# Attention in an 8-expert layer: score passes over 64 keys of two heads, in three units, with the masks as products on GpSimd

## The chip, the core and the metric

The kernel runs on one core of a Trainium2 chip. The core has five engines that work side by side and meet only in semaphores: TensorE (matmuls, results in PSUM banks), ScalarE (activations and copies), VectorE (element-wise work and reductions), GpSimd (element-wise work on SBUF and the indirect DMAs) and SyncE (the queue of plain DMAs). Each works through its own list in order, so an instruction that waits holds up all that stand behind it on its engine. The metric is the device time of one execution in microseconds.

## The reference

One transformer layer on 16 sequences of 256 tokens of width 128: normalised input, causal linear attention with 16 heads, a residual, and a mixture of 8 experts of which each token takes 2 (where both chosen experts have a positive weight, the one with the higher number gives the output). Attention goes in chunks of 64 with a running state, but since the features are all products of two components of q or k, it is the same as a full causal attention with the square of q.k as weight:

```
q = q * f ** (-0.5)
A = jnp.einsum('bhcf,bhsf->bhcs', qi, ki) ** 2 * mask
o = (inter_o + intra_o) / (inter_z + intra_z + EPS)[..., None]   # inter: the same squares over earlier chunks
x = x + attention(layernorm(x)) @ Wo
x = x + experts(layernorm(x))      # gate logits, softmax, top 2 of 8, relu(x w1 + b1) w2 + b2
```

The kernel uses this form: square every score, set those of later keys to zero, multiply by the values extended by a column of ones, and divide by that column.

## The kernel before

**Stages.** First attention for 16 batches (sequences), one a period; then a stage of 39 tiles of 128 rows through the experts. The loop `for p in PERIODS` stands in every engine's code, and each engine takes in it the batches that are its turn: `new` = p is projected, `core` = p-1 is scored, `late` = p-2 is finished and divided, `tail` = p-3 gets its output projection and residual. Pairs of batches are routed: logits when p-4 is even (even periods), the choice when p-5 is even (odd periods), and `scatter` sends a batch's rows to its experts' regions in memory at p-6. No scheduler moves anything: the order of each engine's list is as written.

**Scores.** The 16 heads are two halves (`gg`) of 8; in each, four strips of 32 partitions hold two heads of 16 features, and `k_sb` exists twice, with the features of the one or of the other head set to zero. `score_group(b, g)` (L1085) is one half and one of the two heads of a strip: for each of four strips, 128 keys against 256 queries, and the later 128 keys against the later 128 queries, 384 columns a strip, into the four PSUM banks `sc`. There is one set of those banks: the next group waits in `after(pe, squared, ...)` until ScalarE's `square` (L409) has taken them to SBUF. `mask` (L560) on GpSimd zeroes in 256 of each strip's 384 columns what lies after the query. `weigh` (L1106), A V, adds the four groups into the bank `av`; the first two run in the batch's own period, the last two in the next.

**Around them.** TensorE's list of a period is: scores 0, `project_o(tail)`, `project_q(new)`, scores 1, A V of the batch before (two groups), scores 2, `project_k`, `prefix` (running counts per expert, odd periods), `project_v`, `transpose_xn`, scores 3, two groups of A V. VectorE's is: statistics of two batches ahead (`norm1_stats`, even periods), `residual` and `norm2_stats` of `tail`, the choice, `norm1_apply`, `spread` (a transpose of `av`), `divide` (den, rden, o_sb, oT), `part_k`, `gate_x`, and then either places and slots (odd) or logits, ahead and best (even). GpSimd's is: four masks, with a root (`norm1_root` or `norm2_root`, an addition and a power by -0.5) and two `scatter` DMAs between them. The bank `p7` holds the projected values, the output projection and the counts in turn.

## Time and profile before

| | |
|---|---|
| time, median of 3 runs | 287.44 us (286.88 to 288.08) |
| span of the profiled execution, first to last instruction | 266.1 us |
| outside the span, to the median | 21.3 us |
| TensorE busy | 246.5 us (93%) |
| VectorE busy | 198.0 us (74%) |
| ScalarE busy | 169.0 us (64%) |
| GpSimd busy | 165.9 us (62%) |
| 64 squares on ScalarE | 92.8 us |
| 64 masks on GpSimd | 71.1 us |

The profiled execution has no time of its own beside its span; the 21.3 us are what lies around the span if that execution took the median. Attention fills the span to about 164 us and the experts the rest from about 179. A busy share is an average over stages, and TensorE's includes matmuls that stream beside each other; what a stage is bound by is read from who waits there. A duration includes what an instruction stood for after it had begun.

### The profile page before, as it was taken

What the parts mean: (1) busy time and instruction counts of PE and PEld (TensorE: products, weight loads), DVE (VectorE), ACT (ScalarE), POOL (GpSimd) and SP (SyncE); (2) the same over time, 40 slices, a digit from 0 to 9 for tenths busy, and PEclk for the clock granted to TensorE, in tenths of its full rate; (3) what the DMA queues carried; (4) which work ended last, traced back from release to release, by engine and by line L of the source; (5) the groups of instructions that cost most, each with busy time, mean ns of one, the idle gap of its engine ahead of it and who ended that gap; (6) DMA issues with size and microseconds to landing.
All of it is one profiled execution on the core that took longest, in us unless ns stands there. A gap on an engine that the chain in (4) does not pass through costs nothing.

```text
span 266.1 us, 9039 instructions
## 1 busy us (share of the span) xinstructions
PE 246.5 (93%) x3072; PEld 198.4 (75%) x3072; DVE 198.0 (74%) x715; ACT 169.0 (64%) x311; POOL 165.9 (62%) x190
## 2 busy tenths in 40 slices
PE   6998999999999999999999998887999999999993
PEld 2676777777776776776677766545989999999992
DVE  4877466786899899899799798669888655555552
ACT  2687776776867777677767767534555665656640
POOL 6265555555876976878766766850577774545455
PEclk9999999999999999999999999999999999999998
DMA  3589999999950000000000000447766479776310
GB/s 86 167 254 309 366 358 360 357 357 354 358 164 23 18 5 24 10 14 23 2 23 21 2 23 22 136 124 177 191 179 186 140 245 271 212 182 202 109 39 10
DMA packets 31692, 40.58 MB, mean 153 GB/s; under 512 B 3442, under 2 KB 24468, under 8 KB 31648
## 3 DMA queue, kind: packets, MB, share of 16 engines
q1 hardware_dynamic: 29376, 35.76, 44.3%
q0 software_dynamic: 2272, 4.25, 4.6%
q8 instruction: 26, 0.43, 0.7%
q14 instruction: 18, 0.15, 0.2%
HBM read 17.98 MB, written 22.48 MB: 152 GB/s over the span
## 4 chain that ended last, share of the span: by engine, by line
PE 64%; ACT 17%; DVE 7%; POOL 5%; issue 4%; DMA 1%; DVEq 1%; POOLq 0%
PE sc L1080 32%; PE p L1080 22%; ACT scores L413 16%; PE av L1080 8%; PE p L1083 3%; POOL expert_rows L591 2%; POOL scores L563 2%; DVE hT L1008 1%; DMA rows<-in_L_attn_hidden_states 1%; POOL out L604 1%; DVE y_sb L1014 0%; DVE logit L764 0%; DVE scaled L762 0%; DVE y_sb L1020 0%; POOL rstd L580 0%
## 5 line engine op out<-in xcount | busy, mean ns | idle before, releaser
L413 ACT ACTIVATE scores<-sc 128x1536 f32<-128x1536 f32 x64 | 92.8, 1451 | 44.8 <-PE sc L1080 44.5
L563 POOL TENSOR_SCALAR_AFFINE_SELECT scores<-scores 128x1024 f32<-128x1024 f32 x64 | 71.1, 1113 | 45.2 <-ACT scores L413 44.5
L1080 PE MATMUL sc<-q_sb,k_sb 32*128 32x256 f32 (+1 forms) x1024 | 59.8, 347 | 9.2 <-ACT scores L413 4.9
L1080 PEld LDWEIGHTS sc<-q_sb,k_sb 32*128 32x128 f32 x1024 | 47.8, 184 | 26.5 <-issue 16.6
L604 POOL DMA_INDIRECT out<-y_sb,xr x39 | 38.5, 987 | 26.1 <-DVE y_sb L1020 21.8
L1080 PE MATMUL av<-scores,v_ext 128*32 128x256 f32 (+1 forms) x1024 | 48.8, 329 | 0.3 <-POOL scores L563 0.2
L513 ACT ACTIVATE hT<-sc,b_sb 128x128 f32<-128x128 f32 x78 | 24.4, 363 | 32.9 <-PE sc L1080 32.9
L1080 PE MATMUL sc<-xwT,w_t 128*128 128x128 f32 x312 | 41.6, 276 | 0.0
L1080 PEld LDWEIGHTS av<-scores,v_ext 128*32 128x32 f32 x1024 | 28.9, 109 | 15.8 <-POOL scores L563 1.0
L1008 DVE TENSOR_SCALAR hT<-sc,b_sb 128x128 f32<-128x128 f32 x78 | 23.8, 347 | 20.9 <-PE sc L1080 18.3
L591 POOL DMA_INDIRECT expert_rows<-rows,slot_i x32 | 32.8, 1024 | 9.9 <-issue 7.3
L1080 PEld LDWEIGHTS sc<-xwT,w_t 128*128 128x128 f32 x312 | 37.9, 192 | 0.1
L1080 PE MATMUL av<-w_sb,hT 128*128 x160 | 22.3, 283 | 0.0
L1080 PE MATMUL p<-w_sb,hT 128*128 x152 | 20.6, 279 | 0.0
L1080 PEld LDWEIGHTS av<-w_sb,hT 128*128 128x128 f32 x160 | 19.4, 191 | 1.3 <-issue 0.2
L506 ACT ACTIVATE xw<-xr 128x128 f32<-128x128 f32 x39 | 19.8, 510 | 0.6 <-DMA xr<-expert_rows 0.6
L1080 PEld LDWEIGHTS p<-w_sb,hT 128*128 128x128 f32 x152 | 18.4, 191 | 0.5
L1080 PE MATMUL p<-xnT,wk_sb 128*128 128x256 f32 x62 | 17.6, 406 | 0.6 <-ACT xnT L425 0.6
L663 DVE TENSOR_SCALAR xn<-rows,mv,rstd 128x128 f32<-128x128 f32 x32 | 16.1, 545 | 2.4 <-POOL rstd L572 2.2
L712 DVE STREAM_TRANSPOSE u_sb<-av 128x512 f32<-128x512 f32 x16 | 11.4, 713 | 7.6 <-PE av L1080 7.5
L1080 PE MATMUL p<-xnT,wq_sb 128*128 128x256 f32 x62 | 16.2, 382 | 0.0
L690 DVE TENSOR_SCALAR k_sb<-p,parity 128x512 f32<-128x512 f32 x15 | 11.1, 738 | 5.8 <-ACT k_sb L436 5.8
(147 smaller groups left out, 333.5 us busy)
## 6 DMA issues: line engine op xcount, KB each, us to landing
expert_rows<-pad_rows SPq DMA_DIRECT2D x11, 1572.0 KB, 17.9
w_t<-in_L_ffn_w SPq DMA_DIRECT2D x39, 256.0 KB, 3.2
xr<-expert_rows SPq DMA_DIRECT2D x39, 65.5 KB, 2.5
rows<-in_L_attn_hidden_states SPq DMA_DIRECT2D x16, 128.0 KB, 2.7
out<-y_sb,xr POOLq DMA_INDIRECT x39, 3.3
b_sb<-in_L_ffn_b SPq DMA_DIRECT2D x1, 512.0 KB, 5.7
expert_rows<-rows,slot_i POOLq DMA_INDIRECT x32, 2.4
wk_sb<-in_L_attn_Wk SPq DMA_DIRECT2D x1, 128.0 KB, 2.5
```

The lines of the kernel that those rows point to most:

```text
L413: nc.scalar.activation(scores[g][:, :, :, :].rearrange("p c a t -> p c (a t)"), sc[:, :, 0:SW], ACT.Square, scale=Q_SCALE).then_inc(square ...
L506: nc.scalar.activation(xw[t % 2][:, :], xr[t % XR][:, 0:D], ACT.Identity, bias=xr[t % XR][:, MEAN:MEAN + 1], scale=xr[t % XR][:, FACTOR:FA ...
L513: ins = nc.scalar.activation(hT[t % HT][:, c * P:(c + 1) * P], up_bank[t % 2][0][:, c * P:(c + 1) * P], ACT.Relu, bias=b1_sb[:, bass.ds(e ...
L563: nc.gpsimd.affine_select(out=scores[g][:, :, 0:2, :], in_=scores[g][:, :, 0:2, :], compare_op=ALU.is_ge, fill=0.0, base=0, pattern=[[0, G ...
L591: nc.gpsimd.indirect_dma_start(out=region, out_offset=bass.IndirectOffsetOnAxis(ap=slot_i[:, b, j:j + 1], axis=0), in_=rows[:, b, j, :], i ...
L604: nc.gpsimd.indirect_dma_start(out=out.rearrange("b l d -> (b l) d"), out_offset=bass.IndirectOffsetOnAxis(ap=xr[t % XR][:, IDCOL:IDCOL + ...
L663: ins = nc.vector.tensor_scalar(xn[b % 2][:, j, :], rows[:, b, j, 0:D], mv1[:, b, j, 0:1], rstd1[:, b, j:j + 1], ALU.subtract, ALU.mult)
L690: nc.vector.tensor_scalar(k_sb[b % 2][1][:, :], p5[:, :], parity[:, 1:2], None, ALU.mult).then_inc(k_ready[1], 1)
L712: nc.vector.transpose(u_sb[:, :, :, :, :].rearrange("p n g r w -> p g n (r w)"), av[:, :].rearrange("p (g n w) -> p g n w", g=NG, w=STRIP) ...
L1008: ins = nc.vector.tensor_scalar(hT[t % HT][:, c * P:(c + 1) * P], up_bank[t % 2][1][:, at:at + P], b1_sb[:, bass.ds(e * FC + c, 1)], 0.0, ...
L1080: return nc.tensor.matmul(o, lhsT=l, rhs=r, start=start, stop=stop)
L1083: return nc.tensor.transpose(o, i, ident[:, :])
```

## The change

- A pass of scores has on its 128 partitions 64 keys of one head and the same 64 keys of the strip's other head, instead of 128 keys of one head. `k_sb` holds both heads' keys side by side per chunk of 64, and `v_ext` has the values of the one head in the upper 64 partitions and of the other in the lower.
- The rows of a batch are stored rolled by 64, so that the chunk order in memory is 1, 2, 3, 0 (`PLACE`); `MEETS` lists the stretch of queries that each chunk of keys meets: 256, 192, 128 and 64 columns. A strip has 640 columns per half instead of 768.
- Three units of scores a batch instead of four groups: 448 columns (half 0, chunks 0, 3, 2), 384 (chunk 1 of both halves), 448 (half 1). The tiles of units 0 and 1 exist twice, that of unit 2 once.
- A V of a batch is one piece, in the next period, between scores 1 and scores 2.
- The mask is a product with `causal`, a 128 x 64 tile of ones and zeros, over the diagonal 64 x 64 blocks only: 768, 512 and 768 elements a partition.
- `project_o` moves from behind scores 0 of the next period to the end of its own, into bank `p5` (the last two batches into `p7`); `project_k` follows `project_q`. `residual` and `gate_x` are first on VectorE, logits come before `part_k`, `norm1_stats` later. Roots come first on GpSimd, scatters one period earlier.
- Values are projected in eight pieces of 64 partitions; `gate_x` and `place_v` work on halves. `Wo` and `Wv` are laid out before the call, and `Wo` comes in one DMA instead of eight.

```diff
@@ tiling @@
-    SW = L + P
+    CH = P // 2
+    NK = L // CH
+    PLACE = [(c - 1) % NK for c in range(NK)]
+    MEETS = [(0, L), (0, L - CH), (CH, L - CH), (2 * CH, L - CH)]
+    UNITS = [[(0, 0), (0, 3), (0, 2)], [(0, 1), (1, 1)], [(1, 0), (1, 3), (1, 2)]]
+    NU = len(UNITS)
+    WIDTH = [sum(MEETS[c][1] - MEETS[c][0] for _, c in unit) for unit in UNITS]
...
-        k_sb = [[sb(f"k_sb{i}{r}", [P, NG * L]) for r in range(2)] for i in range(2)]
-        v_ext = [sb(f"v_ext{i}", [P, NTK, 2, H // 2, STRIP]) for i in range(2)]
-        scores = [sb(f"scores{g}", [P, GH, 3, P]) for g in range(GROUPS)]
+        k_sb = [sb(f"k_sb{i}", [P, NG, NK, 2, CH]) for i in range(2)]
+        v_ext = [sb(f"v_ext{i}", [P, NK, H // 2, STRIP]) for i in range(2)]
+        scores = [[sb(f"scores{u}{i}", [P, GH, WIDTH[u]]) for i in range(2 if u < 2 else 1)] for u in range(NU)]
...
+        projected = [bank[:, 0:NTK * DE].rearrange("p (j d) -> p j d", j=NTK) for bank in (p5, p7)]
+        def output_bank(b):
+            return projected[0 if b < NB - 2 else 1]
...
-        CORE, LATE, TAIL, LOGITS, CHOICE, SEND = 1, 2, 3, 4, 5, 6
+        CORE, LATE, TAIL, LOGITS, CHOICE, SEND = 1, 2, 3, 4, 5, 5
@@ scalar @@
+            def square(b, u):
+                act.wait_ge(scored, NU * b + u + 1)
+                after(act, av_done, b - 1 if u < 2 else b)
+                nc.scalar.activation(unit(b, u)[:, :, :], sc[:, :, 0:WIDTH[u]], ACT.Square,
+                                     scale=Q_SCALE).then_inc(squared, 1)
...
                 square(core, 0)
-                if choice is not None:
-                    exponent(choice)
                 if new is not None:
                     copy_q(new)
+                    part_k(new)
                 square(core, 1)
+                if logits is not None and p < NB:
+                    exponent(logits)
                 square(core, 2)
-                if new is not None:
-                    part_k(new)
-                    place_v(new)
-                square(core, 3)
                 if nxt is not None:
                     copy_xnT(nxt)
+                if new is not None:
+                    place_v(new)
@@ gpsimd @@
-                nc.gpsimd.affine_select(out=scores[g][:, :, 0:2, :], in_=scores[g][:, :, 0:2, :],
-                                        compare_op=ALU.is_ge, fill=0.0, base=0,
-                                        pattern=[[0, GH], [0, 2], [1, P]], channel_multiplier=-1).then_inc(masked, 1)
+                own = diagonal(b, u)
+                nc.gpsimd.tensor_tensor(own, own, not_after(own), ALU.mult).then_inc(masked, 1)
@@ vector @@
+                if tail is not None:
                     residual(tail)
+                if core is not None and core > 0:
+                    gate_x(core)
+                if tail is not None:
                     norm2_stats(tail)
...
                 if nxt is not None and nxt > 1:
                     norm1_apply(nxt)
+                if logits is not None and p < NB:
+                    route_logits(logits)
+                if new is not None and new > 0:
+                    part_k(new)
...
+                if stats is not None and p > 0:
+                    norm1_stats((PAIR * stats, PAIR * stats + 1), ln1_count(PAIR * stats))
...
-                if new is not None and new > 0:
-                    part_k(new)
-                    gate_x(new)
@@ tensor @@
+                for g, c, lo, hi, at in pieces(u):
+                    for n in range(GH):
+                        strip = slice(STRIP * n, STRIP * (n + 1))
+                        last = mm(sc[:, n, at], k_sb[b % 2][strip, g, PLACE[c], :, :].rearrange("p r t -> p (r t)"),
+                                  q_sb[b % 2][strip, g * L + lo:g * L + hi])
...
+                for c in range(NK):
+                    for r in range(2):
+                        last = mm(values[CH * r:CH * (r + 1), c, :], xnT[b % 2][:, c * CH:(c + 1) * CH], wv_sb[:, r, :])
...
             for p in PERIODS:
-                score_group(core, 0)
-                if tail is not None:
-                    project_o(tail)
-                if new is not None and new > 0:
+                score(core, 0)
+                if new is not None:
                     project_q(new)
-                score_group(core, 1)
...
                     project_k(new)
+                else:
+                    weigh(late)
+                score(core, 1)
                 if choice is not None:
                     prefix(choice)
-                if new is not None and new > 0:
+                if new is not None:
+                    weigh(late)
+                score(core, 2)
+                if new is not None:
                     project_v(new)
-                if nxt is not None and nxt > 0:
+                if nxt is not None:
                     transpose_xn(nxt)
...
-                score_group(core, 3)
-                weigh(core, 0)
-                weigh(core, 1)
+                if new is not None:
+                    project_o(late)
```

How the change stands in each engine's list. The names in the rows are those of tiles: `sc` the score banks, `av` the bank of A V, `p` one of the banks p5 to p7, and what follows the arrow is read. First TensorE, around the start of an even period, before:

```order
L1080 MATMUL sc<-q_sb,k_sb 128x256 x4
L1080 MATMUL sc<-q_sb,k_sb 128x128 x4
L1080 MATMUL p<-wo_sb,oT 128x136 x2
L1080 MATMUL p<-xnT,wq_sb 128x256 x2
L1080 MATMUL sc<-q_sb,k_sb 128x256 x4
L1080 MATMUL sc<-q_sb,k_sb 128x128 x4
L1080 MATMUL av<-scores,v_ext 32x256 x4
L1080 MATMUL av<-scores,v_ext 32x128 x4
```

and after the change, from the end of the period before:

```order
L1121 MATMUL p<-wv_sb,xnT 64x72 x8
L1124 MATMUL p<-ident,xn 128x128 x2
L1121 MATMUL p<-wo_sb,oT 128x136 x2
L1121 MATMUL sc<-q_sb,k_sb 128x256 x4
L1121 MATMUL sc<-q_sb,k_sb 128x64 x4
L1121 MATMUL sc<-q_sb,k_sb 128x128 x4
L1121 MATMUL p<-xnT,wq_sb 128x256 x2
L1121 MATMUL p<-xnT,wk_sb 128x256 x2
L1121 MATMUL sc<-q_sb,k_sb 128x192 x8
L1121 MATMUL av<-scores,v_ext 32x256 x4
```

The output projection (from `wo_sb`) stood behind the period's first scores and now stands in front of them.

VectorE, from the last operation of `divide` (oT) to the next residual (`rows<-p,rows`), with the logits of an even period between them, before:

```order
L728 STREAM_TRANSPOSE oT<-o_sb 128x256
L690 TENSOR_SCALAR k_sb<-p,parity 128x512
L705 TENSOR_TENSOR raw_x<-p,std 128x16
L762 TENSOR_TENSOR scaled<-raw,rstd 128x32
L764 TENSOR_TENSOR logit<-scaled,gb_sb 128x32
L765 TENSOR_REDUCE top<-logit 128x4
L768 TENSOR_TENSOR shifted<-logit,top 128x32
L775 TENSOR_TENSOR gap<-logit 128x256
L777 TENSOR_TENSOR ahead<-gap,ties 128x256
L785 TENSOR_REDUCE rank<-ahead 128x32
L786 SCALAR_TENSOR_TENSOR best<-rank,number 128x32
L732 TENSOR_TENSOR rows<-p,rows 128x2x128
```

and after, from the same operation on into an even period:

```order
L763 STREAM_TRANSPOSE oT<-o_sb 128x256
L767 TENSOR_TENSOR rows<-p,rows 128x2x128
L769 TENSOR_TENSOR raw<-p,raw_x 128x16
L740 TENSOR_TENSOR raw_x<-p,std 64x16 x2
L775 BN_STATS stats<-rows 128x6 x2
L779 BN_AGGR rows<-stats 128x2 x2
L691 TENSOR_SCALAR xn<-rows,mv,rstd 128x128 x2
L694 TENSOR_TENSOR std<-ve,rstd 128x2
L797 TENSOR_TENSOR scaled<-raw,rstd 128x32
L799 TENSOR_TENSOR logit<-scaled,gb_sb 128x32
L800 TENSOR_REDUCE top<-logit 128x4
L803 TENSOR_TENSOR shifted<-logit,top 128x32
```

Nothing stands between oT and the residual any more, and the logits follow close behind the statistics (`rows<-stats`) of the same period.

GpSimd, around `norm2_root` (`ve<-rows`, `rstd`), before:

```order
L563 AFFINE_SELECT scores<-scores 128x4x256 x3
L577 TENSOR_SCALAR ve<-rows 128x4
L580 TENSOR_TENSOR rstd<-ve,minus_half 128x4
L563 AFFINE_SELECT scores<-scores 128x4x256
L591 DMA expert_rows<-rows,slot_i 33920x131 x2
```

and after:

```order
L594 TENSOR_TENSOR scores<-scores,causal 128x4x192
L606 TENSOR_SCALAR ve<-rows 128x4
L609 TENSOR_TENSOR rstd<-ve,minus_half 128x4
L594 TENSOR_TENSOR scores<-scores,causal 128x4x192
L594 TENSOR_TENSOR scores<-scores,causal 128x8x64
L620 DMA expert_rows<-rows,slot_i 33920x131 x2
L594 TENSOR_TENSOR scores<-scores,causal 128x4x192
```

The root stood behind the period's masks 0 and 1 and now stands in front of mask 0, behind mask 2 of the batch before; the two scatters stand between masks 1 and 2.

## Rows read from the trace of the kernel before

**Rows 1.** The page: the chain that ended last, by engine, as shares of the span.

```profile
PE 64%; ACT 17%; DVE 7%; POOL 5%; issue 4%; DMA 1%; DVEq 1%; POOLq 0%
```

**Rows 2.** By stretch: length; busy PE, PEld, DVE, ACT, POOL; PEclk, DMA share, GB/s.

```profile
91.32:112.10 20.78, 19.84 (x298) 14.91 (x298) 19.17 (x63) 15.15 (x20) 15.67 (x16) 1.00 0.05 15
```

**Rows 3.** Timeline, TensorE and ScalarE: start, duration, engine, line, operation, tiles, shape, count.

```profile
81.03 0.94 PE L1080 MATMUL sc<-q_sb,k_sb 32*128 32x256 f32 x16 [0.22 <-ACT scores L413]
...
81.90 0.73 PE L1080 MATMUL p<-wo_sb,oT 128*128 128x136 f32 x4
82.02 1.45 ACT L413 ACTIVATE scores<-sc 128x1536 f32<-128x1536 f32 x1 [0.87 <-PE sc L1080]
...
83.62 0.94 PE L1080 MATMUL sc<-q_sb,k_sb 32*128 32x256 f32 x16
...
84.48 1.51 PE L1080 MATMUL av<-scores,v_ext 128*32 128x256 f32 x32
```

**Rows 4.** Timeline of VectorE, the starts between which the blocks are measured.

```profile
94.89 0.15 DVE L798 TENSOR_REDUCE esum<-expo 128x4 f32<-128x32 f32 x1
...
96.30 1.39 DVE L663 TENSOR_SCALAR xn<-rows,mv,rstd 128x128 f32<-128x128 f32 x2
...
103.89 0.87 DVE L651 BATCH_NORM_STATS2 stats<-rows 128x6 f32<-128x128 f32 x4
...
105.09 0.39 DVE L732 TENSOR_TENSOR rows<-p,rows 128x256 f32<-128x256 f32 x1
...
106.28 0.57 DVE L663 TENSOR_SCALAR xn<-rows,mv,rstd 128x128 f32<-128x128 f32 x2
...
106.84 0.72 DVE L712 STREAM_TRANSPOSE u_sb<-av 128x512 f32<-128x512 f32 x1
...
109.96 0.75 DVE L690 TENSOR_SCALAR k_sb<-p,parity 128x512 f32<-128x512 f32 x1 [0.58 <-ACT k_sb L436]
...
110.70 0.22 DVE L762 TENSOR_TENSOR scaled<-raw,rstd 128x32 f32<-128x32 f32 x1
...
111.52 0.42 DVE L775 TENSOR_TENSOR gap<-logit 128x256 f32<-128x256 f32 x1
...
112.88 1.52 DVE L786 SCALAR_TENSOR_TENSOR best<-rank,number 128x32 f32<-128x32 f32 x1
...
162.55 0.18 DVE L821 TENSOR_TENSOR place<-p,base 128x32 f32<-128x32 f32 x1
...
163.68 0.15 DVE L880 TENSOR_SCALAR ntile_i<-base 1x8 int32<-1x8 f32 x1
...
168.97 0.72 DVE L712 STREAM_TRANSPOSE u_sb<-av 128x512 f32<-128x512 f32 x1 [1.10 <-PE av L1080]
...
170.78 0.45 DVE L728 STREAM_TRANSPOSE oT<-o_sb 128x256 f32<-128x256 f32 x1
```

**Rows 5.** Timeline of GpSimd, VectorE beside it, and the page's group of scatters.

```profile
87.20 0.23 POOL L577 TENSOR_SCALAR ve<-rows 128x4 f32<-128x4 f32 x1
...
87.52 1.04 POOL L580 TENSOR_TENSOR rstd<-ve,minus_half 128x4 f32<-128x4 f32 x1
87.69 0.42 DVE L723 TENSOR_TENSOR o_sb<-u_sb,rden 128x256 f32<-128x256 f32 x1
...
98.92 1.10 POOL L563 TENSOR_SCALAR_AFFINE_SELECT scores<-scores 128x1024 f32<-128x1024 f32 x1 [1.31 <-ACT scores L413]
99.02 1.27 DVE L723 TENSOR_TENSOR o_sb<-u_sb,rden 128x256 f32<-128x256 f32 x1
...
174.28 2.16 POOL L563 TENSOR_SCALAR_AFFINE_SELECT scores<-scores 128x1024 f32<-128x1024 f32 x2
174.33 1.10 DVE L762 TENSOR_TENSOR scaled<-raw,rstd 128x32 f32<-128x32 f32 x1 [2.14 <-POOL rstd L580]
...
L591 POOL DMA_INDIRECT expert_rows<-rows,slot_i x32 | 32.8, 1024 | 9.9 <-issue 7.3
```

**Rows 6.** By stretch, as rows 2: the end of the span.

```profile
264.00:266.00 2.00, 0.00 (x0) 0.00 (x0) 0.00 (x0) 0.00 (x0) 0.35 (x1) 0.57 0.01 0
```

281 lines of the change are left out of this document (149 added, 132 removed).

## The prediction, made before the changed kernel was run

> **What bounds the kernel now.** I read the chain of waits first, then the busy shares of two neighbouring periods, then the timeline of one period engine by engine. The chain [rows 1] is TensorE and ScalarE: nearly all of it score matmuls, squares and projections. The window over two attention periods [rows 2] says how tight that is: 20.78 us, TensorE busy 19.84, ScalarE 15.15, but also VectorE 19.17. The timeline [rows 3] shows the loop: scores start at 81.03, their square at 82.02 (0.99 later), it takes 1.45, and the next scores start at 83.62, 0.15 after it ended. The one set of score banks is not refilled before ScalarE has emptied it, so a period is four such turns, about 10.3 us. VectorE is the engine to watch. It is 92% busy, part of it standing: the product o_sb starts at 99.02, 0.10 after a mask on GpSimd, and takes 1.27 where another takes 0.42; scaled at 174.33, 0.05 after a mask began, takes 1.10 instead of the 0.22 at 110.70, just past the mask's 1.08 [rows 4, 5]. A VectorE operation on two SBUF inputs that meets a mask waits for its end. A power on GpSimd does not do that (87.52 to 88.56, with the 0.42 product inside it).
>
> The Trainium skill, "SBUF — State Buffer", section "SBUF: two separate sides", says that VectorE (a 2-port mode or two SBUF inputs) and GpSimd take their shared ports as an exclusive lock for a whole instruction. By that rule, the masks above agree and the power (1.04 us) does not. By the rule to the letter the power would stop xn in even periods as well, about 0.5 us each, and the sum would be 299; by the rows it does not.
>
> **The change, part by part.** Period p's clock starts (0) with scores of unit 0.
>
> *TensorE and ScalarE.* Three turns instead of four, 448, 384 and 448 columns a strip instead of 4 x 384. A square of 1536 elements takes 1.45 [rows 3]; one of 1792 takes 1.69 if all of that grows, and I take 1.65 for a fixed part. A wider unit's matmuls take 0.22 more if a 64-column pass costs as much as one of 128, 0.11 if not; I take 0.22. Unit 0: square from 1.21 to 2.86. Unit 1 starts at 3.0, where the eight passes of q and k also end, and its square ends at 5.45. Then the whole A V: before, half of it takes 1.51 [rows 3]; 5120 instead of 6144 columns and one tail less give 2.3. It starts 0.87 after unit 1's scores, so unit 2 starts at 6.2, later than ScalarE asks, its square ends at 9.05, and scores could start at 9.2 (9.5 where prefix stands in front of A V). By this loop alone a pair of periods is 18.7, 2.1 less than now.
>
> *Project_o and residual are now back to back.* Before, between oT and residual VectorE does k_sb, raw_x and the routing, while project_o runs after the next scores. Now TensorE's last work of a period is project_o of the batch whose oT VectorE has just made, and VectorE's next instruction is its residual. Both engines wait for each other: 0.73 of matmuls [rows 3] and hand-overs. I take 0.75 from oT to the next scores and residual 0.15 after those. Queued behind the waiting project_o are the next scores, and for them wait ScalarE and GpSimd.
>
> *VectorE's work*, in blocks by differences of starts [rows 4]. A, residual to statistics: 1.19, and 0.19 for gate_x in two halves of 64 partitions, 1.38. B, xn and std: 0.56. C, scaled to shifted: 0.82. D, k_sb: 109.96 to 110.70 less 0.08 for the raw_x between, 0.66. G, gap to best: 1.36 + 0.22. F, statistics of two batches ahead: 1.20. S, spread and divide, where nothing holds them: 168.97 to 171.23, 2.26. H, choice: 1.41. R, place to slots: 162.55 to 163.68, 1.13. An even period has A B C D G F S = 8.5, an odd one A H B D R S = 7.4.
>
> *The root.* In even periods logits now come straight after the statistics that their root needs. GpSimd's addition and power take 0.23 + 0.09 + 1.04 [rows 5]; scaled can start about 1.46 after A, and B covers 0.56, so VectorE idles 0.9.
>
> *Masks as products.* Half the elements (768, 512, 768 a partition instead of 4 x 1024), two inputs. The trace has no such product on GpSimd. Nearest row: 1.10 for 1024 elements, one input, 1.08 ns each [rows 5]. Read at that rate once per element, the masks take 0.83 and 0.55; with two reads each, 1.65 and 1.10. I take two reads (a product streams twice the input, and this engine has shown no rate above one element in 1.08 ns); both ends stay in the range.
>
> The Trainium skill, "GPSIMD Engine Reference", section "Elementwise — side-by-side cycle accounting", gives 4497 ns for a 2048-element product of two fp32 inputs, the reason being one read port for both. By that figure an estimate is 1.69 and 1.12, and the sum comes within 0.5 us of mine; no run here shows it yet.
>
> *Even period laid out.* Residual 0.15, A to 1.53, power ends 2.94. Mask 0's square is done at 2.86, so the mask goes right behind the power, 3.0 to 4.65, just when scaled is released: the meeting of 174.28 and 174.33 [rows 5]. Scaled ends 4.69, C 5.29, D 5.95. Mask 1 from 5.55 to 6.65 holds gap to 6.93; G ends 8.05, F 9.25, the transpose of spread 9.99. The two scatters (1.02 each and 0.2 to 0.3 idle, 2.5 [rows 5]) run 6.65 to 9.1, mask 2 to 10.75, den ends 10.79, oT 12.07. Next scores 12.8. *Odd period.* A, H to 2.94, where mask 0 (2.95 to 4.6) catches xn; std 4.8, D 5.46, then mask 1 holds picked to 6.68, slots 7.4, oT 9.64, next scores 10.4, over the loop's 9.5. A pair: 23.2. In the last two even periods F is absent; then o_sb meets mask 2, ends 11.05, scores at 12.25: pair 22.65.
>
> *Sum.* Routing runs from the fourth period on: four pairs at +2.4 (9.8 in all) and two at +1.9 (3.7): +13.5. Against it: the first period has three turns for four, -1.5 (2.6 less the wider units and a start that waits for both halves of k); the two periods before routing run at 9.35 instead of 10.3, -1.9; the last period and the way to the experts lose one turn of 2.6 but gain the whole last A V, -1.7. The single Wo load replaces eight while TensorE has other work: nothing, and if that cover were gone 0.5 at most. The expert stage is unchanged. +13.5 - 5.1 = +8.4. The trace's span is 266.1, 21.3 below the median of 287.4; I carry this over: 274.5 + 21.3 = **296**.
>
> **Rivals.**
> *The products stream at one read per element.* Masks 0.83 and 0.55; scaled ends 3.9, gap is free, only ahead and den wait: even 12.0, odd 9.6; without F 10.2. Four pairs +0.8, two -1.0, sum +1.2 - 5.1: 283.5. For it: half the elements. Against it: two inputs.
> *A product on GpSimd does not hold VectorE*, as the power did not [rows 5]. Then even 10.6, odd 9.5 (8.7 + 0.75 without F): -6.6 - 5.1 = -11.7: 275.7. Against it: its reads last as long as the mask's, the power's are four elements.
> *The score loop alone decides*, as now: pairs 18.7, -12.6 - 5.1: 269.7. Against it: VectorE's 19.17 of 20.78 is already more than 18.7 has.
> *Slower still: TensorE's clock falls.* In the even period TensorE has nothing from about 8.4 to 12.2, 3.8 us. Before, matmuls follow each other closely in a period and the clock is full there, 1.00 [rows 2]. Its work ends at about 261.6 and the window 264 to 266 shows 0.57 of full [rows 6], the level of 1.2 GHz for most of it. If it falls in four of the even periods, project_o and the first scores of the next take up to twice as long, about 1 us each: 300. It decides only if an idle stretch of 3.8 us is enough.
> The Trainium skill, "TensorE: Matmul & The Clock Gate", section "HAM oscillation — how this bites in real kernels", would have such idle stretches lower the clock each time; by that rule too 300, and the trace agrees as far as its one drop at the end.
>
> **How the numbers follow.** Forecast (two reads, held ports, full clock) 0.42; clock falls as well 0.14; one read 0.20; no hold 0.13; loop alone 0.11. What a measurement of this kernel can tell from no change is 0.5%, 1.4 us. Slower takes the first two nearly whole, 0.54; of the one-read case a third lies within (rates between one read and two), with a little of the first: same 0.09; faster 0.37. The likeliest's own range is 290 to 300: the masks between 1.4 and 1.8, and 0.3 either way per period in my hand-overs. The 8-in-10 range reaches from 274 to 301.
>
> **What would show it.** Scores of neighbouring periods 12 to 13 and 10 to 10.5 us apart; mask products of 1.6 and 1.1; scaled and xn standing over 1 us beside them; TensorE waiting for oT, and VectorE for project_o, every period; no long wait of TensorE for a square. It is wrong if mask products take under 1 us, if VectorE's products keep their 0.2 to 0.4 beside a mask, or if VectorE waits for A V.

## The result and the profile after

The changed kernel took 317.7 us (median of 4; 312.95 to 320.46), the kernel before 287.8 (286.9 to 290.3) in the same job: 1.09 times as long, 95% interval 1.080 to 1.100. Two later jobs gave 1.112 (1.102 to 1.122) and 1.107 (1.095 to 1.119). Forecast was 296, range 274 to 301: the direction was right, the size was not (+8.4 forecast, +26 to +32 by the three ratios). The profiled run was the fastest of the four, 312.95, with a span of 311.2.

The two periods that answer to [rows 2], one with logits (even) and the next (odd), in the columns of that group:

```profile
94.40:109.55 15.15, 9.57 (x159) 7.31 (x159) 11.94 (x33) 7.70 (x12) 11.19 (x10) 0.92 0.04 11
109.55:122.51 12.96, 11.43 (x165) 8.64 (x164) 7.64 (x33) 6.20 (x6) 5.24 (x5) 0.83 0.04 12
```

This pair is 28.11, against 20.78 in [rows 2] and 23.2 in the forecast; the pair before it is 27.8 and the one behind it 27.75, so the mean of the three is 27.9. TensorE was busy 19.84 of 20.78; now it is 9.57 of 15.15 in the even period, and the granted clock, 1.00 in [rows 2], is 0.92 and 0.83. The chain of the page, which answers to [rows 1]:

```profile
PE 53%; DVE 25%; issue 8%; ACT 5%; POOL 4%; another core or an unknown queue 4%; DVEq 0%; ACTq 0%; POOLq 0%
```

VectorE has come onto it with a quarter, and "another core or an unknown queue" with 4%, most of it in the experts. The even period from scaled to the next scores, all engines (start, duration, engine, what ended the idle time before):

```profile
97.81 1.81 POOL L594 TENSOR_TENSOR scores<-scores,causal 128x768 f32<-128x768 f32 x1
97.85 1.82 DVE L797 TENSOR_TENSOR scaled<-raw,rstd 128x32 f32<-128x32 f32 x1 [0.95 <-POOL rstd L609]
...
99.94 1.27 POOL L594 TENSOR_TENSOR scores<-scores,causal 128x512 f32<-128x512 f32 x1 [0.32 <-ACT scores L439]
100.15 1.10 DVE L803 TENSOR_TENSOR shifted<-logit,top 128x32 f32<-128x32 f32 x1
100.58 1.16 PE L1121 MATMUL sc<-q_sb,k_sb 32*128 32x256 f32 x24
...
101.38 1.09 POOL L620 DMA_INDIRECT expert_rows<-rows,slot_i  x1 [0.17 <-issue]
...
102.32 0.44 PE L1124 MATMUL p<-ident,xn 128*128 128x128 f32 x2
...
102.77 0.96 POOL L620 DMA_INDIRECT expert_rows<-rows,slot_i  x1 [0.30 <-issue]
...
103.38 1.66 ACT L439 ACTIVATE scores<-sc 128x1792 f32<-128x1792 f32 x1 [1.86 <-remote]
...
105.13 1.79 POOL L594 TENSOR_TENSOR scores<-scores,causal 128x768 f32<-128x768 f32 x1 [1.40 <-ACT scores L439]
...
105.47 1.50 DVE L754 TENSOR_SCALAR den<-u_sb 128x32 f32<-128x32 f32 x1
...
107.84 0.45 DVE L763 STREAM_TRANSPOSE oT<-o_sb 128x256 f32<-128x256 f32 x1
...
108.34 1.27 PE L1121 MATMUL p<-wo_sb,oT 128*128 128x136 f32 x4 [5.58 <-DVE oT L763]
```

There are three things to see. The masks hold VectorE as foreseen: scaled 1.82 instead of the 0.22 of [rows 4], shifted 1.10, den 1.50. Then the scores of unit 2 end at 101.74 and ScalarE is free from 101.52, but their square starts at 103.38, 1.64 late; the profile names no engine as its releaser ("remote"), and two scatters run on GpSimd meanwhile. The late square makes a late mask 2 (105.13), and that one catches den. Last, TensorE has nothing from 102.76 to 108.34 (5.6 us). Its granted clock is at half, 1.2 GHz, from 107.2 to 114.0, so project_o takes 1.27 instead of the 0.73 of [rows 3], and the next scores 2.09 instead of 1.16.

The square of unit 2 is 0.4 to 1.7 late in ten of the eleven periods from batch 4 on, where scatters run, and in none before them.

### The profile page after: what moved, and what is told of

It is laid out like the page before. It is cut to its first block, busy times and chain, and to the rows that moved or that the text cites. A ratio compares the mean times of both kernels' runs of the same rounds, so it can differ in the third digit from the quotient of the medians.

```text
span 311.2 us, 9369 instructions
## 1 busy us (share of the span) xinstructions
PE 250.4 (80%) x3254; PEld 203.2 (65%) x3254; DVE 203.9 (66%) x733; ACT 158.2 (51%) x295; POOL 173.4 (56%) x178
## 4 chain that ended last, share of the span: by engine, by line
PE 53%; DVE 25%; issue 8%; ACT 5%; POOL 4%; another core or an unknown queue 4%; DVEq 0%; ACTq 0%; POOLq 0%
PE sc L1121 22%; PE p L1121 16%; PE av L1121 13%; DVE scaled L797 3%; DVE den L754 2%; PE p L1124 2%; DVE u_sb L747 2%; POOL rstd L609 2%; DVE k_sb L722 2%; DVE o_sb L758 2%; ACT v_ext L470 1%; ACT scores L439 1%; DVE oT L763 1%; DVE stats L679 1%
## 5 line engine op out<-in xcount | busy, mean ns | idle before, releaser
L439 ACT ACTIVATE scores<-sc 128x1792 f32<-128x1792 f32 (+1 forms) x48 | 76.5, 1593 | 74.9 <-PE sc L1121 65.5
L594 POOL TENSOR_TENSOR scores<-scores,causal 128x768 f32<-128x768 f32 (+1 forms) x48 | 78.5, 1637 | 62.7 <-ACT scores L439 62.6
L1121 PE MATMUL sc<-q_sb,k_sb 32*128 32x128 f32 (+3 forms) x1024 | 55.7, 346 | 9.7 <-ACT scores L439 5.5
L1121 PEld LDWEIGHTS sc<-q_sb,k_sb 32*128 32x128 f32 x1024 | 43.7, 197 | 24.3 <-issue 16.1
L1121 PE MATMUL av<-scores,v_ext 128*32 128x256 f32 (+3 forms) x1024 | 40.6, 308 | 0.5 <-issue 0.5
L620 POOL DMA_INDIRECT expert_rows<-rows,slot_i x32 | 32.3, 1008 | 11.2 <-issue 7.1
L1121 PE MATMUL p<-wo_sb,oT 128*128 128x136 f32 x64 | 13.9, 349 | 29.0 <-DVE oT L763 27.7
L1121 PEld LDWEIGHTS av<-scores,v_ext 128*32 128x32 f32 x1024 | 26.5, 112 | 11.1 <-issue 4.2
L1121 PEld LDWEIGHTS p<-wo_sb,oT 128*128 128x128 f32 x64 | 10.5, 225 | 32.5 <-DVE oT L763 30.7
L1121 PE MATMUL p<-xnT,wq_sb 128*128 128x256 f32 x62 | 21.9, 486 | 0.0
L722 DVE TENSOR_SCALAR k_sb<-p,parity 128x512 f32<-128x512 f32 x15 | 11.3, 751 | 15.9 <-ACT k_sb L462 14.8
L1124 PE MATMUL p<-ident,xw 128*128 128x128 f32 x39 | 11.4, 292 | 10.9 <-ACT xw L531 10.4
L1121 PEld LDWEIGHTS p<-w_sb,hT 128*128 128x128 f32 x152 | 18.7, 193 | 0.8 <-issue 0.5
```

The source lines that it names most:

```text
L439: nc.scalar.activation(unit(b, u)[:, :, :], sc[:, :, 0:WIDTH[u]], ACT.Square, scale=Q_SCALE).then_inc(squared, 1)
L594: nc.gpsimd.tensor_tensor(own, own, not_after(own), ALU.mult).then_inc(masked, 1)
L620: nc.gpsimd.indirect_dma_start(out=region, out_offset=bass.IndirectOffsetOnAxis(ap=slot_i[:, b, j:j + 1], axis=0), in_=rows[:, b, j, :], i ...
L722: nc.vector.tensor_scalar(k_sb[b % 2][:, :, :, 1, :], by_chunk(p5[:, :]), parity[:, 1:2], None, ALU.mult).then_inc(k_ready[1], 1)
L1121: return nc.tensor.matmul(o, lhsT=l, rhs=r, start=start, stop=stop)
L1124: return nc.tensor.transpose(o, i, ident[:, :])
```

## Experiments: the changed kernel, one thing at a time

**Scatters last.** GpSimd's order:

```diff
-                if send is not None and p < NB:
-                    scatter(send)
                 mask(core, 2)
+                if send is not None and p < NB:
+                    scatter(send)
```

> The changed kernel with GpSimd's two scatters of a period behind the last mask instead of in front of it. In the changed kernel the square of unit 2 starts 0.9 to 1.7 us after its scores end, in ten of the periods with scatters and in none without. Theory L (a signal of TensorE that falls into the first 0.2 to 0.6 us of a scatter arrives late): the squares of unit 2 start 0.07 after their scores again, the gap that they caused goes from both kinds of period, about 1.3 us in ten periods; time 300 to 305, against 313 to 320 of the changed kernel. Rival W (the square waits for something else of the new order, its single score buffer or the exponent in front of it): the lag stays and the time is within 3 us of the changed kernel's, 312 to 319. Rival S (signals are late wherever scatters stand): another wait on TensorE, of the residual or of scores 0, becomes 1 us or more late, 308 to 318.

330.0 us (ratio 1.144, 1.134 to 1.153): slower, outside all three cases. No square of unit 2 waits for a late signal any more. Between squares of unit 0 an odd period is 10.0 to 11.3, but an even one, after the first, 17.3 to 18.7. The scatters now stand in front of the root:

```profile
97.81 1.09 POOL L620 DMA_INDIRECT expert_rows<-rows,slot_i  x1 [0.16 <-issue]
99.20 0.96 POOL L620 DMA_INDIRECT expert_rows<-rows,slot_i  x1 [0.30 <-issue]
...
100.53 1.04 POOL L609 TENSOR_TENSOR rstd<-ve,minus_half 128x4 f32<-128x4 f32 x1
101.56 3.03 POOL L594 TENSOR_TENSOR scores<-scores,causal 128x768 f32<-128x768 f32 x2
101.60 1.82 DVE L797 TENSOR_TENSOR scaled<-raw,rstd 128x32 f32<-128x32 f32 x1 [3.19 <-POOL rstd L609]
103.45 1.19 DVE L799 TENSOR_TENSOR logit<-scaled,gb_sb 128x32 f32<-128x32 f32 x1
...
105.12 0.23 ACT L446 ACTIVATE expo<-shifted 128x32 f32<-128x32 f32 x1 [3.11 <-DVE shifted L803]
105.25 1.65 ACT L439 ACTIVATE scores<-sc 128x1792 f32<-128x1792 f32 x1
```

VectorE waits 3.19 for the root, then stands beside two masks in a row. Behind it ScalarE waits 3.11 with the exponent, which stands in front of the square of unit 2: that square starts 1.6 to 2.1 after its scores in even periods, for this reason now. And the lateness has moved rather than gone: in four even periods the scores of unit 1 end inside or just behind a scatter, and their square is 0.42 to 0.61 late, a smaller form of the expectation's rival S. So the lateness goes where the scatters go, and what is queued ahead of the root is paid in full.

**Masks as single-input selects**, over the same elements:

```diff
-                nc.gpsimd.tensor_tensor(own, own, not_after(own), ALU.mult).then_inc(masked, 1)
+                nc.gpsimd.affine_select(out=own, in_=own, compare_op=ALU.is_ge, fill=0.0, base=CH,
+                                        pattern=[[0, GH], [0, own.shape[2]], [1, CH]],
+                                        channel_multiplier=-1).then_inc(masked, 1)
```

> The changed kernel with each mask an affine select with one input over the same elements (768, 512, 768 a partition) instead of a product with two; the triangle is then right for half the partitions alone, so the output is not the reference's. Theory M (the length of the masks and VectorE's standing beside them carry the even period, as the prediction had it): masks take 0.83 and 0.55, scaled, shifted and den lose 0.9, 0.5 and 0.6 of their standing, an odd period 0.5; about 2.2 us a pair and with the light periods 13 us in all: 299 to 305. Rival C (the late signals and the fallen clock carry the excess over 23.2 us a pair, the masks are a minor term): 308 to 314.

304.3 (three runs at 304 to 306, one at 299.2). By shape, selects first, then the products of the changed kernel:

```profile
L594 POOL TENSOR_SCALAR_AFFINE_SELECT scores<-scores 128x768 f32<-128x768 f32 x32 | 29.1, 912 | 55.7 <-ACT scores L439 55.7
L594 POOL TENSOR_SCALAR_AFFINE_SELECT scores<-scores 128x512 f32<-128x512 f32 x16 | 10.8, 675 | 32.4 <-ACT scores L439 32.4
```

```profile
L594 POOL TENSOR_TENSOR scores<-scores,causal 128x768 f32<-128x768 f32 x32 | 57.9, 1810 | 48.0 <-ACT scores L439 48.0
L594 POOL TENSOR_TENSOR scores<-scores,causal 128x512 f32<-128x512 f32 x16 | 20.6, 1289 | 14.6 <-ACT scores L439 14.6
```

Two inputs take twice the time of one, 1.81 and 1.29 against 0.91 and 0.68, near the 1.65 and 1.10 of the prediction's two reads. The Trainium skill, "GPSIMD Engine Reference", section "Elementwise — side-by-side cycle accounting", has 4497 ns for 2048 elements, measured there for an addition of two inputs. By it an estimate is 1.69 and 1.12; the measurement is 0.12 to 0.17 above that. The median is in theory M's range. But its three middle pairs are 25.7, 24.6 and 23.2, so 2.1 to 4.5 less and not an even 2.2, squares were up to 1.9 late here too, and TensorE's idle stretches were under 2.8: this run does not show that the masks are the largest part.

**Filler.** TensorE kept busy in even periods:

```diff
                 if new is not None:
+                    if pair_of(p, LOGITS) is not None:
+                        pe.wait_ge(k_ready[1], new + 1)
+                        stay_busy(18, p5[:, :])
                     project_o(late)
```

> The changed kernel with 18 matmuls of 512 columns in bf16 (0.21 us each at the full clock, 3.8 us) in the even periods, written to the bank of the keys after VectorE has read them and before project_o, so that TensorE does not stand for 5.6 us there. Theory C (the clock falls because of that idle stretch, and its cost is on the path): the granted clock stays at 1.00 through the attention, project_o takes 0.73 instead of 1.27 and scores 0 1.16 instead of 2.09, the odd period shrinks from 12.9 to 11.5 and the pair by 2; time 8 to 11 lower, 303 to 310. Rival D (the scores and projections at the half clock lie beside VectorE's own work, which sets the period): clock 1.00, but the time is 0 to 4 lower.

307.8 (1.068, 1.060 to 1.075); repeated at the end with

> The changed kernel with 18 filler matmuls in even periods, which keep the clock at 1.00 through the attention. Where the kernel before takes 287 to 290: 306 to 309, a pair 24.45, as measured. Where it takes 268 to 270 and signals are on time: even 13.05, odd 10.48, a pair 23.5, as measured with no scatters, time 276 to 281, against the 274.5 of span plus 1.7 that the prediction's steps give for such a run.

it was 307.6 (302.3 to 308.3). The same two periods:

```profile
94.20:108.15 13.95, 12.91 (x177) 8.60 (x176) 11.66 (x33) 7.01 (x9) 11.08 (x10) 1.00 0.05 16
108.15:118.64 10.49, 9.26 (x165) 7.07 (x164) 9.09 (x31) 6.73 (x8) 5.37 (x5) 1.00 0.03 9
```

Clock 1.00, and a pair is 24.44: 3.7 less, where theory C expected 2 (3.4 on the mean of three pairs, 24.5). The odd period is 10.49, the 10.4 of the forecast; with the clock full its square 2 is on time as well, because the scores no longer end inside a scatter. The whole gained less than the periods because this profiled run's clock was first granted in full at 23.5 us, against 4.8 in the changed kernel's; its first period took 15.7 between squares, not 11.8. That varies from run to run of one kernel: in the first repeat of the changed kernel the clock was full at 5.4, fell back from 8.8 to 22.5, and the first period took 15.8.

What the fallen clock costs is paid largely on VectorE. In the changed kernel it stands for ScalarE's part of `k_sb` in the four odd periods behind a fallen clock, 1.9 to 2.9 us each (before: 0.6), since the projections and the copy come late:

```profile
115.50 0.75 DVE L722 TENSOR_SCALAR k_sb<-p,parity 128x512 f32<-128x512 f32 x1 [2.28 <-ACT k_sb L462]
```

With the filler there is no such wait in the odd periods.

**Project_o behind the next scores 0.**

```diff
                 score(core, 0)
+                if of(p, TAIL) is not None:
+                    project_o(of(p, TAIL))
                 if new is not None:
                     project_q(new)
...
-                if new is not None:
-                    project_o(late)
```

> The changed kernel with project_o of a batch behind the next period's scores 0 instead of ahead of them, everything else in place. Theory H (the hand-over oT, project_o, scores, residual stands on the path in every period, 0.75 each, and TensorE's idle stretch ends earlier, so the clock falls less): scores 0 no longer wait for oT, 14 periods gain 0.75 and more where the clock is half; 300 to 307. Rival V (VectorE is the bound in even periods: its residual waits for scores 0 and project_o, and comes no earlier): the gain is in the light and the last periods alone, 309 to 316. The other side: the residual now comes 1.2 later after oT, and the period grows by it, 315 to 330.

323.2 (1.119, 1.106 to 1.131): the time of the other side. Between squares of unit 0, even periods are 10.4 and odd ones 16.8. The next scores 0 no longer wait for oT, so the even period ends early; but in the odd one the projections of q and k are queued behind project_o, which waits for the oT of the even one, and for them ScalarE:

```profile
110.89 1.27 PE L1121 MATMUL p<-wo_sb,oT 128*128 128x136 f32 x4 [4.34 <-DVE oT L763]
...
113.91 0.59 ACT L456 COPY q_sb<-p 128x512 f32<-128x512 f32 x1 [5.64 <-PE p L1121]
```

A pair is 27.2, not longer than the changed kernel's 27.9, so the expected reason (every period longer) did not come. What this variant loses, it loses in the last four routing periods: they take 54.5, against 44.1 in the changed kernel's first trace and 47.9 and 48.0 in its repeats.

## Experiments: late signals

**The kernel before with its later tiles at other addresses.**

```diff
+        pad = sb("pad", [P, 2496])
```

> The kernel before with an unused SBUF tile of 2496 floats a partition behind its score tiles, which is what the changed kernel's tiles grew by: every later tile, those of the expert stage too, gets another address, nothing else changes. In the changed kernel and its three variants tiles 8 to 16 of the expert stage take 14 us more than before with the same instructions: VectorE and ScalarE stand up to 5 to 7 us for signals of TensorE while GpSimd issues a string of indirect DMAs. Theory A (the place of the tiles brings this): 296 to 302. Rival P (it is the momentary order and phase of the engines, which here stay as before): 286 to 289, as the kernel before.

286.8 against 289.7 (ratio 0.993, 0.988 to 0.998): moving these tiles did not add time. But its trace changed the reading of everything. Its span is 286.2, not 266.1, and late squares, which had been taken for the changed kernel's own, are in it too. First the attention, then the experts:

```profile
92.72 0.94 PE L1081 MATMUL sc<-q_sb,k_sb 32*128 32x256 f32 x16 [0.22 <-ACT scores L414]
92.72 1.13 POOL L592 DMA_INDIRECT expert_rows<-rows,slot_i  x1 [0.30 <-issue]
...
94.39 1.45 ACT L414 ACTIVATE scores<-sc 128x1536 f32<-128x1536 f32 x1 [1.56 <-PE sc L1081]
```

```profile
197.58 1.15 PE L1081 MATMUL av<-w_sb,hT 128*128 x8
...
198.57 1.06 PE L1081 MATMUL sc<-xwT,w_t 128*128 128x128 f32 x8
...
199.97 0.96 POOL L592 DMA_INDIRECT expert_rows<-rows,slot_i  x1 [0.30 <-issue]
...
202.53 0.99 POOL L605 DMA_INDIRECT out<-y_sb,xr  x1 [0.30 <-issue]
...
204.69 0.29 DVE L1021 TENSOR_TENSOR y_sb<-av,y_sb 128x128 f32<-128x128 f32 x1 [5.21 <-remote]
205.01 0.62 ACT L514 ACTIVATE hT<-sc,b_sb 128x128 f32<-128x128 f32 x2 [6.23 <-remote]
```

Scores end at 93.65 inside a scatter, and their square starts 0.74 later instead of 0.06. In the experts VectorE and ScalarE stand 5.2 and 6.2 us while six scatters follow each other from 196.04 on; the matmuls that they go on with had ended 6.0 and 5.4 earlier, at 198.73 and 199.63. A pair of periods is 22.0 here. The trace behind rows 1 to 6 has the same instructions and none of this: there the scores of the same batch, too, end 0.93 into a scatter, and their square starts 0.06 later. Of the 20 us between the two traces 6.4 lie in the attention and 13.5 behind the first square of the last batch, nearly all in the experts. The kernel before, timed in seven jobs, had medians of 287.8 to 289.7 in six, on at least four chips (spans of 284 to 292 in this one), and 268.7 in one, on a chip of its own, with spans of 266 to 271. So the 21.3 us that the prediction put around the span lie inside it: only 1.7 to 1.9 are outside.

**The changed kernel with no scatters in the attention, without and with filler.**

```diff
-                if send is not None and p < NB:
-                    scatter(send)
...
+            for b in range(NB - 4):
+                scatter(b)
             norm2_root(NP - 1)
```

> The changed kernel with all scatters of routed rows taken out of the attention stage and issued after it (so the way to the experts is longer and the total means nothing; read the periods). Theory L (TensorE's signals are late while GpSimd issues scatters): no square of unit 2 is late, mask 2 comes 1.4 earlier and leaves den alone; even period 13.9 at most instead of 15.2, odd 11.4 instead of 12.9 with the clock still falling, a pair 24 to 25.5. Rival W (the square is late for a reason of its own): still 0.9 to 1.7 late, a pair 27.5 to 28.2.

> The same with the 18 filler matmuls of the filler variant as well (pair there 24.45: even 13.96, odd 10.48). If late signals and clock add up, the even period loses the 1.0 of lateness that was left, 12.8 to 13.3, which is the prediction's 12.8, the odd period stays at 10.4 to 10.5, a pair 23.2 to 23.8. If the even period is VectorE's chain whatever square 2 does, 13.9 stays.

340.1 and 328.9; only the periods count. No square was late in either. Without filler three pairs took 25.2, 24.3 and 25.9, the clock falling to half in every even period still, in or behind idle stretches of TensorE of 3.4 to 4.3 us. With it:

```profile
89.82:102.87 13.05, 12.91 (x178) 8.59 (x177) 10.76 (x33) 6.96 (x9) 8.10 (x8) 1.00 0.00 1
102.87:113.35 10.48, 9.25 (x165) 7.06 (x164) 9.08 (x31) 6.73 (x8) 4.20 (x3) 1.00 0.01 2
```

13.05 and 10.48, against 12.8 and 10.4 laid out in the prediction. The four corners of a pair, each the mean of the same three pairs, are 27.9 (as changed; 27.5 in each of its repeats), 25.1 (no scatters), 24.5 (full clock) and 23.5 (both). Taking the scatters out also frees GpSimd of them, 2.4 us a period, so that corner is late signals and scatters together.

**Select and filler.** The edits of the two variants together.

> Filler and single-input selects together (the triangle right for half the partitions alone, so the output is not the reference's). Masks 0.91 and 0.67 as in the select variant. If the masks' hold on VectorE and the clock are separate costs, even 12.3, odd 9.9: a pair 22.2 instead of 24.45, 2.2 x 4 + 1.5 x 2 = 12 us off the 307.8 of the filler variant: 294 to 298. If the idle and hand-overs of VectorE, not the masks, set the pair: 302 to 306.

299.7 (1.039, 1.027 to 1.051), between the two cases. Pairs are 23.3 (even 12.65, odd 10.66), 1.1 less than with filler alone and not 2.2, one even period was 14.3, where the clock fell once, and this run had its full clock from 4.6 us on, which the filler variant had not. The squares of unit 2 were late in both kinds of period here, by 1.3 and 1.9, and with filler alone in one, by 1.0. So of the masks' second input 1.1 a pair is what was seen with the clock full, with more lateness against it; its worth by itself was not measured.

**The kernel before with its scatters apart.**

```diff
                 if send is not None and p < NB:
-                    scatter(send)
+                    scatter(send, (0,))
                 if core is not None:
                     mask(core, 3)
+                if send is not None and p < NB:
+                    scatter(send, (1,))
```

> The kernel before with the two scatters of a period apart: one behind mask 2 as now, the other behind mask 3. In the trace of the kernel before with a moved tile (span 286.2) the scores of the next unit end 0.93 into the second of two scatters that follow each other, and their square starts 0.74 late, every period with scatters takes 10.97 instead of 10.3. Theory L (a signal of TensorE that falls into a scatter is late): each scatter now ends before the next scores do, no square is late, ten periods at 10.3 to 10.5: 280 to 283. Rival (the late squares belong to something else, or another signal takes their place): 286 to 290.

284.4 against 288.0: ratio 0.978 (0.971 to 0.985). That is below 1 beyond the noise, though not by a clear 2%, and the time lies between the two cases of the expectation. Between squares of unit 0 every period from the second on is 10.28 to 10.50, as in the trace behind rows 1 to 6, where the moved-tile variant had 10.97 to 11.2 in the periods with scatters. Only in the last batch, where scatters still follow each other, two squares are late, by 1.2 and 1.0. The chain has gone back to [rows 1]:

```profile
PE 65%; ACT 17%; POOL 5%; DVE 4%; issue 4%; another core or an unknown queue 3%; DMA 1%; DVEq 0%; ACTq 0%; POOLq 0%
```

The 3% under "another core" are the experts, which this edit leaves alone.

**The same in the changed kernel**, one scatter in front of mask 1 and one behind it, and a **combination** with filler and with VectorE's statistics of the batches ahead put in front of scaled:

> The changed kernel with the two scatters of a period apart, one in front of mask 1 and one behind it, nothing else. Theory L: scores 2 end between them, so square 2 starts on time; the even period falls from 15.2 towards the 14.4 to 14.8 that it had with no scatter, the odd one from 12.9 to 11.3; but mask 1 comes 1.3 later and holds VectorE somewhere else. A pair 25.5 to 26.5, time 306 to 311. Rival (any scatter near a signal costs the same, wherever it is): 313 to 318.

> The changed kernel with scatters apart, the 18 filler matmuls, and the statistics of the batches ahead moved into VectorE's idle time in front of scaled. With filler and no scatters a pair took 23.5 (even 13.05, odd 10.48). If the root's idle 0.95 is used, the even period is 12.3 to 12.8 and a pair 22.8 to 23.3, 5 to 7 us less than the filler variant's 24.45 a pair gave in all: 299 to 303. If scatters apart only move the lateness: 305 to 309. Faster than the kernel before (287 to 290) in neither case.

The first: 318.5 (one run at 311.3, three at 317 to 321), pairs of 25.3, 26.4 and 26.8 and no late square, but its times scatter too widely to be told from the changed kernel's. The combination: 327.0 (1.130, 1.122 to 1.138), slower and against both cases. In the even period the filler outlasted the wait that it was to fill:

```profile
109.76 4.05 PE L1123 MATMUL p<-ones 128*128 128x512 bf16 x18
109.91 0.45 DVE L765 STREAM_TRANSPOSE oT<-o_sb 128x256 f32<-128x256 f32 x1
...
113.65 0.63 PE L1123 MATMUL p<-wo_sb,oT 128*128 128x136 f32 x4
```

oT was ready at 110.36 and project_o came at 113.65. But that is the smaller part: even periods are 13.4 to 14.4, near the 13.95 with filler alone. The loss is in the odd periods, all but the first 15.6 to 15.8 where the filler variant had 10.48:

```profile
121.58 1.09 POOL L620 DMA_INDIRECT expert_rows<-rows,slot_i  x1 [2.59 <-DVE slot_i L885]
121.95 2.08 DVE L756 TENSOR_SCALAR den<-u_sb 128x32 f32<-128x32 f32 x1
122.70 1.28 POOL L594 TENSOR_TENSOR scores<-scores,causal 128x512 f32<-128x512 f32 x1
...
124.45 2.83 DVE L760 TENSOR_TENSOR o_sb<-u_sb,rden 128x256 f32<-128x256 f32 x1
125.18 1.81 POOL L594 TENSOR_TENSOR scores<-scores,causal 128x768 f32<-128x768 f32 x1
...
127.81 1.27 PE L1123 MATMUL p<-wo_sb,oT 128*128 128x136 f32 x4 [5.02 <-DVE oT L765]
```

The scatter that now stands in front of mask 1 waits 2.59 for the slots, which VectorE makes late in an odd period. Masks 1 and 2 come behind it and hold den and o_sb, 2.08 and 2.83; TensorE stands 5.0 for oT where there is no filler, and the clock falls after all.

**Scatters apart in even periods, statistics ahead, no filler.**

> The changed kernel with two edits of order and no filler: the statistics of the batches ahead in VectorE's idle time in front of scaled, and in even periods one scatter in front of mask 1 and one behind it (odd periods as they were, both between mask 1 and mask 2). In the combined variant oT of an even period was ready 11.2 after its residual began, and TensorE was still busy with the filler for 3.3 us: it was the filler's fault that the variant was slower. If that reading is right, TensorE stands under 2 us there, the clock stays at 1.00 in most periods, even 11.1 to 12, odd 10.5 to 11.3 and a pair 22 to 23: 294 to 302. If the clock falls anyway or the signals are late again, a pair is 25 or more and the time 306 to 315.

303.9 where the kernel before took 268.7 (1.123, 1.114 to 1.131), in the one job without late signals. No square was late here, though scores ended inside a scatter six times. A pair is 26.9, against my 22 to 23: with the statistics gone from between them, scaled meets mask 0, and shifted the scatter and mask 1; TensorE stands 5.5, the clock falls again, and the even period is 15.7:

```profile
96.43 1.82 POOL L594 TENSOR_TENSOR scores<-scores,causal 128x768 f32<-128x768 f32 x1
96.64 1.66 DVE L799 TENSOR_TENSOR scaled<-raw,rstd 128x32 f32<-128x32 f32 x1
...
98.43 1.09 POOL L620 DMA_INDIRECT expert_rows<-rows,slot_i  x1 [0.18 <-issue]
...
98.78 2.10 DVE L805 TENSOR_TENSOR shifted<-logit,top 128x32 f32<-128x32 f32 x1
...
99.55 1.28 POOL L594 TENSOR_TENSOR scores<-scores,causal 128x512 f32<-128x512 f32 x1
```

Shifted starts 0.77 before mask 1, inside the scatter, and stands until mask 1 has ended. Beside a scatter with no mask coming right behind it the same operation took its 0.19. So a variant of the changed kernel loses to the kernel before without late signals too.

**The changed kernel again**, twice:

> The changed kernel as it is. The last job ran where the kernel before takes 268.7, as in the trace read for the prediction (span 266.1), and its variant of the changed kernel showed no square late beside scatters; the jobs before ran where it takes 287 to 290 and squares and expert tiles are late. If the kernel before takes 287 to 290 here as well, the changed kernel is at 312 to 319 again, even periods 15.2, odd 12.6 to 13, tiles 8 to 16 of the experts slow. If it takes 268 to 270 here: with no late signals, but the clock falling in the idle stretch, a pair is 25 to 26 (25.1 was measured with no scatters) and the time 287 to 292; if a clean pair is the prediction's 23.2, 275 to 279.

> The changed kernel as it is, once more. Where the kernel before takes 287 to 290 in the same job: 313 to 320, unit 2's squares up to 1.7 late beside scatters. Where it takes 268 to 270: no square late, the clock still falling in the idle stretch of even periods, a pair 25 to 26 and the time 287 to 292; 275 to 279 if the clean pair is the prediction's 23.2.

320.1 and 318.3 against 288.4 and 288.3, the first 1 us above what was expected of it. Neither job met the other condition, so the changed kernel itself has no time there.

## Why the prediction was wrong

By its own steps, against the moved-tile trace (span 286.2), which is the kernel before as it was timed; the changed kernel's profiled span is 25.0 longer.

1. *Score loop alone, 9.2 to 9.5.* Right: the two periods before routing are 9.36 and 9.31.
2. *Project_o and residual back to back.* Right in kind: TensorE waits for oT 27.7 us in 13 places, VectorE for project_o 14.3 in 13. But the stretch of TensorE's waiting in an even period is 5.6 and not 3.8.
3. *Root idle 0.9.* 0.95 before scaled. Two waits of VectorE were missing: for place_v (up to 1.15 before raw_x in the routing periods), a copy that is now last on ScalarE, and for `k_sb`, 1.9 to 2.9 in four odd periods.
4. *Products of 1.65 and 1.10 that hold VectorE.* 1.81 and 1.29, and they hold it.
5. *Even 12.8, odd 10.4, a pair 23.2.* Right only with a full clock and without the scatters: 23.5. As the kernel is, 27.9. **This is the step that failed**, in the word "full": the clock falls. I had it as a rival at 0.14, with the rule of the Trainium skill, "TensorE: Matmul & The Clock Gate", section "HAM oscillation — how this bites in real kernels", and this trace agrees with it: the clock went to half at each of TensorE's four idle stretches of 4 to 6 us in the attention, and once more, at 151.5, where no stretch was over 2. But I priced it at about 1 us in each of four even periods. By the corners of the pair it costs 1.6 alone and 3.4 with the scatters in; the scatters with their late signals cost 1.0 at the full clock and 2.8 at the fallen one. The two feed each other: with a late square TensorE's idle stretch in an even period is 5.6 and not 4.0 to 4.3, the clock is at half for 6.8 behind each and not for 3.4 or 6.8, and at half the clock the odd period's scores end inside a scatter, where at the full clock they do not. How much of the scatters' share is lateness, and how much the time that they take on GpSimd, was not separated; with the scatters apart and no square late a pair was still 26.2 on the mean.
6. *The sum.* The twelve routing periods grew by 23.5, from 131.0 to 154.5, not by 13.5, from 124.6 to 138.1. It is the eight with statistics behind the logits that failed: 110.4 instead of 92.8; the last four took 44.1 instead of 45.3. The baseline was 6.4 too low as well, by its late signals. Start and first period took 2.5 more, not 1.5 less: unit 1 now needs the second half of q and k, and its scores start 4.5 after those of unit 0 where I had 3.0; the rest of that 2.5 is not taken apart. From the last period on 1.0 more, not 1.7 less. 2.5 - 1.9 + 23.5 + 1.0 = 25.1.
7. *266.1 and 21.3.* The trace read was of an execution without late signals, the times were of executions with them. I called the difference "around the span" with no row for it. No run shows such a term: the runs have 1.7 to 1.9 outside the span. The +8.4 did not use the 21.3, but it was reckoned from a pair of 20.78 where the kernel as timed had 22.0, and 20 us of waiting in the timed kernel were nowhere in my rows.

The named rivals below the forecast (one read, no hold, loop alone) are excluded by what stands in 2 to 4.

Open: what makes TensorE's signals late beside scatters, and why in all jobs but one. Shown is that they go when the scatters go, and move when the scatters move, in both kernels, and that moving the kernel's later tiles by 2496 floats did not change the time. All the clock's shares above are of a pair of periods; what the experts gain or lose by it was not measured.

## What to carry to other kernels

When a trace's span and the times of the same kernel differ by more than the few us that other runs have outside the span, stop and find the missing time before forecasting. Where a change makes one engine wait for another's last product, price the idle stretch twice: once as waiting, and once as the clock that falls behind it, through all that the next period's first work releases. Fill or reorder only after asking what is queued behind, and what the moved instruction itself waits for: four of these variants (scatters last, project_o behind, scatters apart in the changed kernel, the combination) were slower or no better for an edit that removed the very wait it aimed at.

## What was not expected of the hardware

- Where signals are late, they are so by place: in the thirteen traces of that condition with scatters in the attention, of both kernels and their variants, scores ended inside an indirect scatter of GpSimd, with ScalarE free, 94 times, and 86 of the squares started over 0.3 us later (0.35 to 1.9). Of 346 that ended outside one, after the first scatter, 11 were late, all within 0.35 us behind a scatter. In the other condition (the trace behind rows 1 to 6 and the last scatters-apart variant) 13 ended inside a scatter and none was late. In a string of scatters in the experts two signals came 5.4 and 6.0 late (205.01 and 204.69 above).
- The same kernel took 268.7 in one job and 287.8 to 289.7 in the others. The two traces of it differ in late signals, and in the clock that falls behind them in the experts.
- The clock of TensorE was first granted in full at 4.6 to 23.5 us after the start, for the same first instructions; with the latest one the first square came 2.2 later and the first period was 3.9 longer.
- A product of two inputs on GpSimd took twice a select of one (1.81 against 0.91 for 768 elements).
- A VectorE operation that starts inside a scatter with a mask coming right behind it stood until the mask had ended: shifted took 2.10 in five periods of the last scatters-apart variant, den 2.0 to 2.2 in the combination. Inside a scatter alone shifted took 0.19, 37 times in eleven traces.
